# A recommender tower on one core: the first fields copied by two engines and listed over two queues

## The reference

```python
e = stack([tbl_f[ids[:, f]] for f in range(32)], axis=1)        # 1024 x 32 x 16
x0 = xk = e
for W in (W0, W1, W2):                                          # 32 x 32 x 64, then 32 x 64 x 64 twice
    xk = relu(einsum('bmd,bhd,mhk->bkd', x0, xk, W))
    outs.append(sum(xk, axis=2))                                # 64 columns each
h = concatenate([concatenate(outs, 1), dense_ctx], axis=1)      # 1024 x 208
h = relu(h @ W_top1 + b_top1); h = relu(h @ W_top2 + b_top2)    # 512, then 256
y = h @ W_top3                                                  # 1024 x 1
```

## Time and profile before

| | us |
|---|---|
| median of 3 runs | 650.54 |
| lowest, highest | 650.01, 652.65 |
| span of the profiled execution | 646.9 |
| PE busy | 587.2 (91%) |
| DVE busy | 584.8 (90%) |
| ACT busy | 358.1 (55%) |
| POOL busy | 470.5 (73%) |

### The profile page before, as it was taken

One profiled execution on the slowest core, in us unless ns is written; L12 is line 12 of the kernel. 1 busy time (PEld: TensorE's weight loads), 2 busy tenths in 40 slices (PEclk: granted clock), 3 DMA queues, 4 the chain that ended last, 5 costly groups with the idle time before them and its releaser, 6 DMA issues.

```text
span 646.9 us, 7779 instructions
## 1 busy us (share of the span) xinstructions
PE 587.2 (91%) x2896; PEld 209.9 (32%) x2896; DVE 584.8 (90%) x329; ACT 358.1 (55%) x594; POOL 470.5 (73%) x405
## 2 busy tenths in 40 slices
PE   0078898999898989999999999999999999999998
PEld 0023332333232323333334323333334323333455
DVE  1039897999999999999999999999999999999994
ACT  0006472756646564757656575747676465736552
POOL 6677769588888888898888888888989783803011
PEclk9999998999999999999999999999999999999999
DMA  5286585728073643737181735547380826300000
GB/s 161 50 313 165 208 285 147 279 39 304 22 232 131 183 179 73 290 64 296 31 313 22 221 140 146 216 81 281 54 308 4 275 85 199 162 3 2 1 2 1
DMA packets 27138, 96.51 MB, mean 149 GB/s; under 512 B 7414, under 2 KB 12540, under 8 KB 22876
## 3 DMA queue, kind: packets, MB, share of 16 engines
q1 hardware_dynamic: 18908, 93.90, 43.4%
q0 software_dynamic: 8192, 2.11, 2.9%
HBM read 80.25 MB, written 15.73 MB: 148 GB/s over the span
## 4 chain that ended last, share of the span: by engine, by line
DVE 42%; PE 24%; issue 12%; POOL 11%; DMA 8%; SPq 2%; ACT 1%; DVEq 0%; POOLq 0%; ACTq 0%
DVE prod L489 40%; PE acca L590 10%; POOL emb L362 7%; PE accb L590 5%; DMA rows<-field_dram 4%; PE acc L560 3%; POOL prod L380 3%; PE spread L633 2%; DMA field_dram<-zb_field 2%; DMA emb<-in_table,idx 1%; SPq L280 1%; PE accb L611 1%; PE acc L611 1%; DVE prod L470 1%; ACT zb_field L720 1%
## 5 line engine op out<-in xcount | busy, mean ns | idle before, releaser
L362 POOL DMA_INDIRECT emb<-in_table,idx x256 | 247.9, 968 | 81.7 <-issue 67.3
L590 PE MATMUL acca<-prod,w 128*64 128x512 f32 x1024 | 230.4, 597 | 3.5 <-DVE prod L489 2.4
L590 PE MATMUL accb<-prod,w 128*64 128x512 f32 x960 | 216.4, 596 | 13.3 <-DVE prod L489 13.3
L380 POOL TENSOR_TENSOR prod<-rows,mates 128x1024 f32<-128x1024 f32 x70 | 164.3, 2381 | 13.1 <-issue 12.6
L489 DVE TENSOR_TENSOR prod<-rows,x1a 128x2048 f32<-128x2048 f32 x64 | 146.2, 2287 | 6.0 <-PE acca L590 3.0
L489 DVE TENSOR_TENSOR prod<-rows,x1b 128x2048 f32<-128x2048 f32 (+1 forms) x65 | 146.4, 2254 | 4.4 <-PE acca L590 3.7
L489 DVE TENSOR_TENSOR prod<-rows,x2a 128x2048 f32<-128x2048 f32 x64 | 146.3, 2287 | 1.1 <-PE accb L590 0.8
L489 DVE TENSOR_TENSOR prod<-rows,x2b 128x2048 f32<-128x2048 f32 x64 | 146.3, 2287 | 0.0
L590 PEld LDWEIGHTS acca<-prod,w 128*64 128x64 f32 x1024 | 72.0, 138 | 147.2 <-issue 136.3
L590 PEld LDWEIGHTS accb<-prod,w 128*64 128x64 f32 x960 | 65.6, 137 | 155.8 <-issue 113.8
L725 ACT ACTIVATE x1a<-acc 64x512 f32<-64x512 f32 x62 | 35.3, 570 | 128.1 <-PE acc L560 127.4
(11 more groups left out here) (74 smaller groups left out, 258.6 us busy)
## 6 DMA issues: line engine op xcount, KB each, us to landing
rows<-field_dram SPq DMA_DIRECT2D x30, 2048.0 KB, 13.7
field_dram<-zb_field SPq DMA_DIRECT2D x32, 256.0 KB
mates<-field_dram SPq DMA_DIRECT2D x16, 512.0 KB, 3.8
emb<-in_table,idx POOLq DMA_INDIRECT x256
field_dram<-zb_field SPq DMA_DIRECT2D x32, 128.0 KB
field_dram<-zb_field SPq DMA_DIRECT2D x16, 192.0 KB
rows<-field_dram SPq DMA_DIRECT2D x2, 1024.0 KB, 7.3
rows<-field_dram SPq DMA_DIRECT2D x1, 1536.0 KB, 12.8
```

The lines of the kernel that those rows point to most:

```text
L362: pool.indirect_dma_start(out=emb[q % EMBS][:, j * EMB:(j + 1) * EMB], out_offset=None, in_=table, in_offset=bass.IndirectOffsetOnAxis(ap= ...
L380: nc.gpsimd.tensor_tensor(prod0[:, (q * L0 + k) % RING0, :], rows[:, slot(q, t), :], mates[:, :], ALU.mult).then_inc(s_prod0p, 1)
L590: mm = nc.tensor.matmul(acc[j % 2][side * HID:(side + 1) * HID, :], (w1 if layer == 1 else w2)[:, step, :], prod[:, (made(layer, s, half, ...
```

## The change

Seven edits, all in the opening of the kernel:

- The copies of fields 0 are shared: ACT does the first two blocks of 32 partitions, DVE the other two (`turned_parts`, `fields_half`), with a semaphore of their own. Later periods keep four copies on ACT.
- In periods 0, 1 and 2 the five list DMAs are issued by two engines: SP issues parts 0 and 2 and ACT parts 1, 3 and 4 (`SIDES`, `list_side`); ACT does it right behind its copies. From period 3 on SP issues all five, in the order 0, 2, 1, 3, 4.
- POOL no longer waits for the turn of fields 0 before it issues the gathers of period 1.
- `FIRST` becomes 1, 1, 2, 1 and 3 tiles.
- The fifth product of period 0 is made in two halves of 512 columns, each with its semaphore; PE contracts each half as it comes (`layer0_end`), and x1a of subperiod 0 waits for the first half alone.
- The eleventh gather of period 0 (`NEAR`) gets its own semaphore; PE waits for it and runs two rounds of filler ahead of the turn of fields 0. The filler ahead of layer 0 goes from five rounds to four.
- PE's wait for the weights w1 and w2 (loaded by then) moves ahead of that filler.

```diff
...
     GROUPS = [(0, 4), (4, 4)]
-    FIRST = [(0, 2), (2, 2), (4, 1), (5, 3)]
+    FIRST = [(0, 1), (1, 1), (2, 2), (4, 1), (5, 3)]
+    SIDES = ((0, 2), (1, 3, 4))
+    NEAR = 10
     BUFFERS = 3
...
         s_turned, s_field, s_listed = sem("s_turned"), sem("s_field"), sem("s_listed")
+        s_field_v, s_l0c, s_near = sem("s_field_v"), sem("s_l0c"), sem("s_near")
         s_mates = sem("s_mates")
...
         s_first = [sem(f"s_first{t}") for t in range(len(FIRST))]
-        s_prod0v, s_prod0p = sem("s_prod0v"), sem("s_prod0p")
+        s_prod0v, s_prod0p, s_prod0c = sem("s_prod0v"), sem("s_prod0p"), sem("s_prod0c")
         s_prod, s_used = sem("s_prod"), sem("s_used")
...
         block = ctx.enter_context(nc.Block())
+        def list_side(eng, q, side):
+            for j, count, half, first, step, times in [LIST_PARTS[i] for i in SIDES[side]]:
+                to = bass.AP(field_dram.tensor, (q % LISTS * LENGTH + first * 8) * N,
+                             [[HALF, 2 * count], [step * 8 * N, times], [1, HALF]])
+                part = bass.AP(zb_field[:, :].tensor, (FIELD + 2 * j) * N + half * HALF,
+                               [[N, 2 * count], [0, times], [1, HALF]])
+                eng.dma_start(to, part).then_inc(s_listed, 16)
+        def fields_ready(eng, q):
+            eng.wait_ge(s_field, q + 1)
+            if q == 0:
+                eng.wait_ge(s_field_v, 1)
+        def turned_parts():
+            by_d = field[:, :].rearrange("n (f g d b) -> n d g f b", f=2, g=DH // QUAD, b=BT)
+            turned = spread[:, 0:2 * P].rearrange("q (g f b) -> q g f b", f=2, b=BT)
+            return [(by_d[:, d, :, :, :], turned[d * FIELDS:(d + 1) * FIELDS, :, :, :]) for d in range(QUAD)]
         @block.sync
...
             def list_fields(q):
-                sp.wait_ge(s_field, q + 1)
+                fields_ready(sp, q)
                 if q >= LISTS:
                     sp.wait_ge(s_prod, made(1, 2 * (q - LISTS), 0, UNITS - 1))
-                for j, count, half, first, step, times in LIST_PARTS:
-                    to = bass.AP(field_dram.tensor, (q % LISTS * LENGTH + first * 8) * N,
-                                 [[HALF, 2 * count], [step * 8 * N, times], [1, HALF]])
-                    part = bass.AP(zb_field[:, :].tensor, (FIELD + 2 * j) * N + half * HALF,
-                                   [[N, 2 * count], [0, times], [1, HALF]])
-                    sp.dma_start(to, part).then_inc(s_listed, 16)
+                list_side(sp, q, 0)
+                if q >= LISTS:
+                    list_side(sp, q, 1)
                 sp.wait_ge(s_listed, (q + 1) * len(LIST_PARTS) * 16)
...
                         in_offset=bass.IndirectOffsetOnAxis(ap=idx[:, q, j:j + 1], axis=0)
-                    ).then_inc(s_gather[q % EMBS], 16)
+                    ).then_inc(s_near if (q, j) == (0, NEAR) else s_gather[q % EMBS], 16)
             def gather_early(q):
...
             gather_early(0)
-            pool.wait_ge(s_turned, 1)
             gather_early(1)
...
             nc.vector.tensor_tensor(w0[:, :, :], w0[:, :, :], w0_swapped, ALU.add).then_inc(s_w0sum, 1)
+            def fields_half():
+                dve.wait_ge(s_turned, 1)
+                for to, src in turned_parts()[QUAD // 2:]:
+                    last = nc.vector.tensor_copy(to, src)
+                last.then_inc(s_field_v, 1)
             def rows_wait(q, t):
...
                 wait_for(dve, s_l0, q * L0 + k - RING0 + 1)
-                nc.vector.tensor_tensor(prod0[:, (q * L0 + k) % RING0, :], rows[:, slot(q, t), :], mates[:, :],
-                                        ALU.mult).then_inc(s_prod0v, 1)
+                if (q, k) == (0, L0 - 1):
+                    for c, done in ((0, s_prod0c), (1, s_prod0v)):
+                        part = slice(c * HALF, (c + 1) * HALF)
+                        nc.vector.tensor_tensor(prod0[:, k, part], rows[:, slot(q, t), part], mates[:, part],
+                                                ALU.mult).then_inc(done, 1)
+                else:
+                    nc.vector.tensor_tensor(prod0[:, (q * L0 + k) % RING0, :], rows[:, slot(q, t), :], mates[:, :],
+                                            ALU.mult).then_inc(s_prod0v, 1)
             def outer(layer, s, half, u):
...
                     sum_d(zb[0:HID, p * BT:(p + 1) * BT], zin3[third(p), :], EMB, s_zb)
+            fields_half()
             for k in range(L0):
...
                 wait_for(pe, s_act, towers)
-                pe.wait_ge(s_gather[q % EMBS], (q // EMBS + 1) * GATHERS * 16)
+                pe.wait_ge(s_gather[q % EMBS], ((q // EMBS + 1) * GATHERS - (q % EMBS == 0)) * 16)
                 by_d = emb[q % EMBS][:, :].rearrange("b (n d) -> b d n", d=DH)
...
                 contract(acc0, w0[:, k, :], prod0[:, (q * L0 + k) % RING0, :], k == 0, k == L0 - 1).then_inc(s_l0, 1)
+            def layer0_end():
+                k = L0 - 1
+                for c, made_c, done in ((0, s_prod0c, s_l0c), (1, s_prod0v, s_l0)):
+                    pe.wait_ge(made_c, 1 if c == 0 else L0)
+                    nc.tensor.matmul(acc0[c * HID:(c + 1) * HID, :], w0[:, k, :], prod0[:, k, c * HALF:(c + 1) * HALF],
+                                     start=False, stop=True).then_inc(done, 1)
             def outer(j, half, u):
...
             pe.wait_ge(s_ident, 1)
+            pe.wait_ge(s_w12, 32)
+            pe.wait_ge(s_near, 16)
+            keep_busy(acc[1][:, :], 2)
             turn_fields(0, 0)
-            pe.wait_ge(s_w12, 32)
             pe.wait_ge(s_listed, len(LIST_PARTS) * 16)
-            keep_busy(acc[1][:, :], 5)
+            keep_busy(acc[1][:, :], 4)
             pe.wait_ge(s_w0sum, 1)
-            for k in range(L0):
+            for k in range(L0 - 1):
                 layer0(k, 0)
+            layer0_end()
             turn_fields(1, 0)
...
                 wait_for(act, s_listed, q * len(LIST_PARTS) * 16)
-                by_d = field[:, :].rearrange("n (f g d b) -> n d g f b", f=2, g=DH // QUAD, b=BT)
-                turned = spread[:, 0:2 * P].rearrange("q (g f b) -> q g f b", f=2, b=BT)
-                for d in range(QUAD):
-                    last = nc.scalar.activation(by_d[:, d, :, :, :], turned[d * FIELDS:(d + 1) * FIELDS, :, :, :], ACT.Copy)
+                for to, src in turned_parts()[:QUAD // 2 if q == 0 else QUAD]:
+                    last = nc.scalar.activation(to, src, ACT.Copy)
                 last.then_inc(s_field, 1)
+                if q < LISTS:
+                    fields_ready(act, q)
+                    list_side(act, q, 1)
             def relu_twice(to, src, done):
...
                     act.wait_ge(s_prod, made(1, 0 if s == 2 else s - 1, half, UNITS - 1))
-                if half == 0:
+                if (s, half) == (0, 0):
+                    act.wait_ge(s_l0c, 1)
+                    relu_twice(x_of(1, s)[0], layer0_of(s), s_x1[0])
+                elif half == 0:
                     act.wait_ge(s_l0, (s // 2 + 1) * L0)
...
```

## The result

The changed kernel takes 665.63 us (median of four runs, 662.02 to 670.06) against 650.27 for the kernel before (median of four, 648.0 to 652.65): a ratio of 1.025, interval 1.0209 to 1.0291. Ratios leave out executions that a disturbance made longer. The forecast was 648.5 with a range up to 651.0. The profiled execution's span is 661.4, 14.5 more than before.

The account below looks back on a forecast made before the run. DVE was taken as the bound, busy 90%, so the end follows the opening's series up to 118.69. Terms 0.65 + 0.4 - 0.3 + 0.5 + 0.4 + 0.4 make 2.05 less: 648.5 us, range 645.5 to 651.0.

Parts of the forecast that it names:

- Second gathers without a pause: POOL's first gather of period 1 moves from 26.39 to 23.86; costs nothing and brings nothing of its own.
- Copies on two engines: Opening, fields 0: ACT keeps two copies, DVE's two take 0.85; fields ready at 27.05 instead of 27.70, gain 0.65.
- Lists on two queues: Periods 0, 1 and 2: the slow end of each list's transfer at 138 GB/s goes, gain 0.4 per list.
- bound of -0.3: Lower bound per list on two queues: the small parts end alone on ACT's queue for longer.
- first rival: Two list queues bring nothing: gain of 0.85 is left, 649.7 us; chance 0.20.
- What ACT pays: ACT's three list issues take 2.3 us in periods 0 to 2, covered by idle time or later-ending rows.
- my worst case: ACT's three list issues take 3.9 us, if held as long as SP's five were.
- Single tiles, halves: Layer 0, period 0: first product 1.4 earlier but gain 0, loss 0.3 by smaller pieces; last product in halves gains 0.5.
- slower rival: Four filler rounds don't raise PE's clock, layer 0 runs low and ends 3.3 later: 651.8 us; chance 0.08.
- half product's +0.5: Layer 0's end, period 0: first half stands 0.55 earlier, x1a begins then; one more DVE start costs 0.05.
- Fillers: PE, opening: two rounds before the turn, uncounted; four instead of five before layer 0 last from about 33.4 to 40.2.
- the 0.46: Turn of fields 0 falling from 1.13 to 0.67 if fillers raised PE's clock; not counted in the forecast.

Follow-up runs that it names:

- second trace of before: The kernel before, unchanged, profiled again beside the experiments: 650.01 us.
- three-edit kernel: The changed kernel with POOL's pause put back and all lists issued by SP again: 651.11 us in one run, then 1.005 of the kernel before.

## Why the prediction was wrong

- *Second gathers without a pause*: "they cost nothing and bring nothing of their own". This step failed, and it alone makes the result: +15.7 us by itself, in one run. I priced the pause by what the gathers would do earlier, and never asked what the pause did for the turn. The row was there: the chain has the turn's end at 26.13 and the copies at 26.15, with POOL idle from 23.55 on; I took that hand-over as a constant. No rival had it either. What the runs showed in its place: without the pause the copies start 12.1 us behind the turn instead of 0.06, and with it put back into the changed kernel 0.75. Why the signal waits stays open.
- *Copies on two engines*: the size was right. DVE's two took 0.87 (0.85), and the list's first issue came 0.66 earlier than in the second trace of before, 0.48 than in the first (0.65). "DVE has nothing queued behind this" held. But the gain didn't reach the end.
- *Lists on two queues*: sized 0.4 each, measured -0.1 to -0.3 for the first, -0.9 for the second and none for the third. The bound of -0.3 was too near. The first rival was nearest here, though two queues brought a loss and not nothing. The Trainium skill, "DMA: Bandwidth & Descriptors", section "Issuing engines are not separate DMA queues", has such DMAs interleave on the same 16 engines, which puts the term near nothing; the first list agrees (6.96 and 6.88 against 6.73). The second list's loss (8.18 against 7.25) is not what that section states. The dip to 138 GB/s was real but not the one queue's: in the changed kernel, with two queues, there are three microseconds at 195 to 197 GB/s and then one at 117.

```profile
42.00:43.00 1.00, 0.00 (x0) 0.00 (x0) 0.00 (x0) 0.00 (x0) 0.69 (x2) 0.50 1.00 197
...
45.00:46.00 1.00, 0.00 (x0) 0.00 (x0) 0.00 (x0) 0.00 (x0) 0.00 (x0) 0.50 0.81 117
```

- *What ACT pays*: 2.3 was 2.9, below my worst case, and still not covered: with the lists on two queues POOL's halving began 4.4 later than in the unchanged kernel, with the last gathers behind it.
- *Single tiles, halves*: DVE's first product came earlier by the 1.4 forecast beside the copies' 0.66, and the third one hardly (43.25; 43.54 in the unchanged kernel, 43.03 with the copies alone, which is 0.2 of the 0.3 that I put down as a loss). What I missed is PE's idle stretch between them; in the three-edit kernel it made the slower rival's case, layer 0 at the low clock, by another cause than a late rise. The half product's +0.5 can't be seen beside that.
- *Fillers*: leaving the 0.46 out was right: with the same filler ahead of it the turn took 0.68 in two kernels (the changed one, and with the pause back) and 1.09 in four. The granted clock is 1.00 in the turn of all six, so it doesn't tell them apart. By it my "the clock rose some 5.8 us after the start" was wrong too: the earlier trace rows have 1.00 at 37 as at 40, so what made the first fillers slow was not a granted clock at its lower level.
- The range ended at 651.0 and 0.05 stood on slower. I had put down PE's hand-overs as free in every rival, so no case was wider than its own step.

## What to carry to other kernels

A wait that looks like lost time on one engine can go with another engine's prompt signal, as POOL's pause did here: before taking one out, look at which hand-over follows it within a few microseconds and try the edit by itself. An opening gain is only worth what passes the next hand-over; here 2 us at the first product were 0.3 one stage later, with PE idle ahead of a piece that was no faster and then at the lower clock. A sum of seven small edits needs at least one run of each alone.

## What the runs showed of the hardware

- PE's signal at the end of its first turn reached ACT and DVE 8.4 to 14.0 us late in all six kernels in which POOL's gathers ran on through that end, 5.5 and 1.6 late where four or one went ahead of the wait, and 0.1 to 0.8 late in all kernels where POOL paused or worked in that place. At the third turn, with gathers running on, it was anywhere from under 0.7 to 7.1 late.
- What holds it is not settled: it is neither a standing wait of POOL for that signal, nor PE's queue, nor the filler, nor who reads the bank. Data of the last gather that is still moving can't hold it to the end, as it had stopped 1.7 to 2 us before the signal came. The recording may have a part: the first trace of the unchanged kernel, the only one in which all its turns' signals came within 0.05 us, is also the only one with 7624 semaphore updates on record; the other nineteen have 4495 to 4824. No run was made to tell.
- The unchanged kernel's own signals vary: copies 0.06 behind the first turn in one profile, 0.23 in another; x1a's start differed by 0.9 us between them, at spans of 646.9 and 648.2.
- Three DMA issues on ACT took 2.82 to 3.35 us of its time behind its copies, 0.94 to 1.1 each; SP's two beside the first of them took 0.82 in the changed kernel, 0.41 each.
